# Graph attention over 64 graphs: a new order on four engines and in the DMA queue

## The reference, cut to what matters

```
h = relu(layernorm(x))                                   # x: 64 x 128 x 384
q, k, v = h @ Wq + bq, h @ Wk + bk, h @ Wv + bv          # 12 heads of 32
scores = q @ k.T / sqrt(32) + beta * adj                 # adj: 64 x 128 x 128, shared by the heads
scores = where(adj > 0, scores, -9e15)
out = x + softmax(scores) @ v
```

## Time and profile before

| | |
|---|---|
| median of 3 runs | 549.69 us (548.75 to 551.79) |
| the profiled execution's own time | 552.24 us |
| its span, first to last instruction | 550.4 us |
| granted clock of TensorE, mean | 0.991 of full speed |
| busy: PE, DVE, ACT, POOL | 504.8, 469.1, 443.3, 127.4 us |
| moved by DMA | 106.19 MB, mean 193 GB/s |

### The profile page before, as it was taken

How to read it: one execution, slowest core, us unless ns; L and a number is a source line. 1 busy time by engine, 2 the same in 40 slices (tenths; PEclk the granted TensorE clock), 3 DMA queues, 4 the chain that set the end, 5 groups by cost and what they waited for, 6 DMA issues and landing times.

```text
span 550.4 us, 17259 instructions
## 1 busy us (share of the span) xinstructions
PE 504.8 (92%) x5142; PEld 417.6 (76%) x5142; DVE 469.1 (85%) x2323; ACT 443.3 (81%) x1816; POOL 127.4 (23%) x204
## 2 busy tenths in 40 slices
PE   8998897887999989899998989989898999999986
PEld 7776776765887878688787878868786887888774
DVE  5687697967899899889989989889997998887796
ACT  3567687786697969879796997879798797989885
POOL 5411021212122222212222222222222221111131
PEclk9999999999899999989999999999999999999999
DMA  8424465656577667767766775776667566644311
GB/s 256 155 88 153 132 222 164 214 194 210 168 231 232 222 214 231 231 184 231 233 221 219 239 226 174 234 234 221 219 230 233 172 197 213 193 154 149 107 59 58
DMA packets 111959, 106.19 MB, mean 193 GB/s; under 512 B 12448, under 2 KB 97312, under 8 KB 111904
## 3 DMA queue, kind: packets, MB, share of 16 engines
q1 hardware_dynamic: 111904, 105.56, 59.6%
HBM read 55.84 MB, written 49.68 MB: 192 GB/s over the span
## 4 chain that ended last, share of the span: by engine, by line
SPq 30%; DMA 27%; PE 18%; DVE 8%; issue 7%; ACT 1%; DVEq 0%
DMA out_rows<-out_blocks 14%; SPq L425 12%; DMA probs_rows<-probs_blocks 10%; SPq L454 7%; PE G_ps L906 7%; SPq L401 6%; PE S_ps L975 4%; SPq L416 3%; DMA probs_moved<-probs_rows 3%; PE S_ps L927 2%; DVE probs L737 2%; PE PT_ps L959 2%; PE PT_ps L943 2%; SPq L393 1%; ACT probs L538 1%
## 5 line engine op out<-in xcount | busy, mean ns | idle before, releaser
L538 ACT ACTIVATE probs<-probs,negmax 128x128 f32<-128x128 f32 x532 | 206.1, 397 | 0.0
L737 DVE CUSTOM_DVE_ANT_0 probs<-S_ps,bias 128x128 f32<-128x128 f32 x768 | 166.1, 285 | 17.7 <-PE S_ps L927 17.4
L553 ACT ACTIVATE probs_blocks<-probs,negmax 128x128 f32<-128x128 f32 x236 | 92.0, 392 | 77.2 <-DVE negmax L737 67.1
L509 POOL TENSOR_TENSOR w_raw<-w_raw,x_ring 128x384 f32<-128x384 f32 x63 | 64.0, 1017 | 312.7 <-DVE w_raw L757 312.7
L906 PE MATMUL G_ps<-h_hi,w_hi 128*128 128x512 f32 x288 | 119.6, 415 | 0.0
L906 PE MATMUL G_ps<-h_hi,w_lo 128*128 128x512 f32 x288 | 118.6, 412 | 0.0
L906 PE MATMUL G_ps<-h_lo,w_hi 128*128 128x512 f32 x288 | 117.2, 407 | 0.0
L538 ACT ACTIVATION_READ_ACCUMULATOR probs<-probs,negmax 128x1 f32 x532 | 104.9, 197 | 0.0
L927 PEld LDWEIGHTS S_ps<-qk 32*128 32x128 f32 x1536 | 50.9, 189 | 38.0 <-issue 36.6
L927 PE MATMUL S_ps<-qk 32*128 32x128 f32 x1536 | 63.7, 294 | 15.7 <-DVE h_lo L676 10.4
L943 PE MATMUL PT_ps<-probsT,v 128*32 128x128 f32 x1512 | 54.7, 277 | 20.2 <-DVE probsT L778 13.9
(11 more groups left out here) (60 smaller groups left out, 725.6 us busy)
## 6 DMA issues: line engine op xcount, KB each, us to landing
probs_rows<-probs_blocks SPq DMA_DIRECT2D x59, 256.0 KB, 3.1
probs_moved<-probs_rows SPq DMA_DIRECT2D x236, 64.0 KB, 2.0
out_dram<-w_raw SPq DMA_DIRECT2D x63, 192.0 KB, 2.9
x_ring<-in_x_dram SPq DMA_DIRECT2D x61, 192.0 KB, 2.8
out_rows<-out_blocks SPq DMA_DIRECT2D x29, 384.0 KB, 3.3
w_raw<-out_rows SPq DMA_DIRECT2D x116, 96.0 KB, 2.2
xhat_rows<-xhat_blocks SPq DMA_DIRECT2D x26, 384.0 KB, 2.5
xhat_moved<-xhat_rows SPq DMA_DIRECT2D x104, 96.0 KB, 2.7
```

The source lines that it names most:

```text
L509: nc.gpsimd.tensor_tensor(y[:, place, :], y[:, place, :], x_ring[:, bass.ds(at, D)], ALU.add).then_inc(y_ready, 1)
L538: last = nc.scalar.activation(p, p, ACT.Exp, bias=negmax[:, e, j * KC + m:j * KC + m + 1], scale=TURN, accum_out=rowsum[:, e, m * HC + j:m ...
L553: last = nc.scalar.activation(blocks[:, j, :, :], probs[:, a, j, 0, :].rearrange("p (c e) -> p c e", c=HC), ACT.Exp, bias=negmax[:, a, j * ...
L737: last = nc.vector.tensor_tensor_reduce(probs[:, a, j, m, :], S_ps[:, j, m * N:(m + 1) * N], bias[(z.par + 1) % 2][:, z.s, :], 1.0, LARGES ...
```

## The change

It does these things:

- SP: the four reads of `out_rows` move from the end of an odd slot to the next even slot, behind the four reads of `probs_rows`. The four reads of xhat blocks are split, two in each slot (`READS`). One x load moves from s = 2 to s = 1. The write of xhat rows stands behind the reads of xhat blocks.
- PE: the scores come first in every slot, then the first projection stretch, then the product with v (before: product with v directly behind the scores, and ahead of them where s = 0). In a group's last slot (`closing`) the second stretch comes ahead of the values, too.
- DVE: it stores no unit. `add_bv` moves to behind the mask terms, in the closing slot to behind `h_lo`; the quotient and the transpose of probs' blocks are last in the slot; the mask comes ahead of `store_outT` in every slot.
- ScalarE: it stores the sixth unit as well (`STORE_Q`), and `high_part` comes directly behind the exponentials of probs_blocks.

```diff
@@ -41,3 +41,5 @@
-LOADS = [[0], [1], [2, 3], []]
+LOADS = [[0], [1, 2], [3], []]
+READS = [[0, 1], [2, 3], [0, 1], [2, 3]]
 QK_UNITS = 6
@@ -48,8 +50,7 @@
-STORE_1 = [[], [1], [], [4]]
-STORE_2 = [[0], [], [3], []]
 STORE_0 = [[], [], [2], []]
-STORE_V = [[], [], [], [5]]
+STORE_1 = [[], [1], [], [4]]
+STORE_Q = [[], [], [], [5]]
+STORE_2 = [[0], [], [3], []]
@@ -176,4 +177,3 @@
         qk_in_psum = sem("qk_in_psum")
-        qk_stored_act, qk_stored_dve = sem("qk_stored_act"), sem("qk_stored_dve")
+        qk_stored = sem("qk_stored")
         mask_ready, bias_ready = sem("mask_ready"), sem("bias_ready")
@@ -230,2 +230,5 @@
                 first_f = n == NG and s == 0
+                self.pairs_before = 4 * (n - 1) + s - 2 > 0
+                self.first_f = first_f
                 self.moved = [2] * (not self.F and 4 * (n - 1) + s - 4 >= 0) + [2, 1] * first_f
@@ -235,3 +238,4 @@
-                self.scores_first = self.A and self.P and s > 0
+                self.closing = self.P and s == GROUP - 1
                 self.par = off % 2
...
@@ -394,6 +390,6 @@
-            def read_blocks(pair):
+            def read_blocks(pair, columns):
                 at = pair * HC * RUN
-                for c in range(HC):
+                for c in columns:
                     came = xhat_rows[pair, :, c * RUN:(c + 1) * RUN].rearrange("(r p) n -> p r n", r=HC)
@@ -425,13 +421,21 @@
                         sp.dma_start(goes, came).then_inc(probs_blocks_moved[(z.s - 1) % 2], 16)
+                if z.W and z.s % 2 == 0 and z.pairs_before or z.first_f:
+                    sp.wait_ge(out_rows_written, 16 * z.pairs_written())
+                    for b in range(HC):
+                        came = out_rows[z.s // 2, :, b * SIX:(b + 1) * SIX].rearrange("(j p) n -> p j n", j=HC)
+                        goes = out_moved[b * HD:(b + 1) * HD, z.s // 2, :].rearrange("p (j n) -> p j n", j=HC)
+                        sp.dma_start(goes, came).then_inc(out_blocks_moved[z.s // 2], 16)
                 load_ahead(z)
-                if not (z.static and not 1 <= z.groups(0) <= NG - 3):
-                    if z.s % 2 == 1:
-                        sp.wait_ge(xhat_ready, order(z.count(2)) + 1)
-                        write_rows(z.s // 2)
-                    if z.s == 2:
-                        sp.wait_ge(rows_written[0], 16 * z.groups(0))
-                        read_blocks(0)
+                xhat_here = not (z.static and not 1 <= z.groups(0) <= NG - 3)
+                if xhat_here and z.s == 2:
+                    sp.wait_ge(rows_written[0], 16 * z.groups(0))
+                if xhat_here and z.s >= 2:
+                    read_blocks(0, READS[z.s])
                 if z.M and z.s == 0:
                     sp.wait_ge(rows_written[1], 16 * z.groups(-1))
-                    read_blocks(1)
+                if z.M and z.s < 2:
+                    read_blocks(1, READS[z.s])
+                if xhat_here and z.s % 2 == 1:
+                    sp.wait_ge(xhat_ready, order(z.count(2)) + 1)
+                    write_rows(z.s // 2)
                 if z.W and z.s % 2 == 1:
@@ -448,8 +452,2 @@
                     sp.dma_start(out[bass.ds(z.o - d, 1), :, :].rearrange("b t d -> t (b d)"), y[:, place, :]).then_inc(out_written[place], 16)
-                if z.W and z.s % 2 == 1:
-                    sp.wait_ge(out_rows_written, 16 * (z.pairs_written() + 1))
-                    for b in range(HC):
-                        came = out_rows[1 - z.s // 2, :, b * SIX:(b + 1) * SIX].rearrange("(j p) n -> p j n", j=HC)
-                        goes = out_moved[b * HD:(b + 1) * HD, 1 - z.s // 2, :].rearrange("p (j n) -> p j n", j=HC)
-                        sp.dma_start(goes, came).then_inc(out_blocks_moved[1 - z.s // 2], 16)
                 if z.L:
@@ -567,9 +565,8 @@
                     act.wait_ge(scores_in_psum, z.count(-1) - z.s)
-                stored = qk_stored_dve if u == QK_UNITS - 1 else qk_stored_act
                 if u < KC:
                     nc.scalar.activation(qk[z.par][:, u, :], G_ps[:, u % 2, :], ACT.Identity, bias=bq_scaled[:, u:u + 1],
-                                         scale=TURN * SCALE).then_inc(stored, 1)
+                                         scale=TURN * SCALE).then_inc(qk_stored, 1)
                 else:
                     nc.scalar.activation(qk[z.par][:, u, :], G_ps[:, u % 2, :], ACT.Identity,
-                                         bias=bk_col[:, u - KC:u - KC + 1]).then_inc(stored, 1)
+                                         bias=bk_col[:, u - KC:u - KC + 1]).then_inc(qk_stored, 1)
@@ -611,2 +608,7 @@
                     exponentials_ahead(z)
+                if z.M:
+                    high_part(z)
+                if z.P:
+                    for u in STORE_Q[z.s]:
+                        store_qk(z, u)
                 if z.E and not z.F:
@@ -617,6 +619,4 @@
                     store_probsT(z, 2)
-                if z.M:
-                    high_part(z)
                 if z.P:
-                    for u in STORE_2[z.s] + STORE_V[z.s] * (z.static and z.groups(0) == 0):
+                    for u in STORE_2[z.s]:
                         store_qk(z, u)
...
@@ -813,7 +799,5 @@
                     return
-                if z.F and z.A:
-                    mask(z)
                 if z.O and not z.F:
                     reciprocals(z)
-                if z.scores_first:
+                if z.A:
                     mask(z)
@@ -821,4 +805,2 @@
                     store_outT(z)
-                if z.A and not z.F and not z.scores_first:
-                    mask(z)
                 if z.M:
@@ -829,8 +811,7 @@
                     reciprocals(z)
-                for d in z.moved:
-                    quotient(z, d)
-                if z.A:
+                if z.F:
+                    for d in z.moved:
+                        quotient(z, d)
+                if z.F and z.A:
                     add_bv(z)
-                if z.R:
-                    transpose_probs(z)
                 if z.F and z.A:
@@ -861,2 +842,4 @@
                         mask_terms(z)
+                        if z.A and not z.closing:
+                            add_bv(z)
                     statistics(q, s)
@@ -872,5 +857,9 @@
                     normalise(z, q)
-                if z.P and not first:
-                    for u in STORE_V[z.s]:
-                        store_qk(z, u)
+                if z.A and z.closing:
+                    add_bv(z)
+                if not z.F:
+                    for d in z.moved:
+                        quotient(z, d)
+                if z.R:
+                    transpose_probs(z)
                 if first and z.s == GROUP - 1:
@@ -899,7 +888,4 @@
-                    if u == 1:
-                        if started(z.stored_dve()):
-                            pe.wait_ge(qk_stored_dve, z.stored_dve())
-                    elif started(z.stored_act(u - 2)):
-                        pe.wait_ge(qk_stored_act, z.stored_act(u - 2))
+                    if started(z.units(u - 1)):
+                        pe.wait_ge(qk_stored, z.units(u - 1))
                 for n in range(first, last):
@@ -918,3 +904,3 @@
                 if z.s == 0:
-                    pe.wait_ge(qk_stored_act, z.stored_act(-2))
+                    pe.wait_ge(qk_stored, z.units(0))
                 ts = slice(z.s * N, (z.s + 1) * N)
@@ -922,4 +908,2 @@
                 for m in range(KC):
-                    if z.s == 0 and m == KC - 1:
-                        pe.wait_ge(qk_stored_dve, z.stored_dve())
                     for j in range(HC):
@@ -1027,7 +1011,3 @@
                         warm(WARM[GROUP])
-                if z.A and z.scores_first:
-                    scores(z)
-                if z.O:
-                    probs_times_v(z)
-                if z.A and not z.scores_first:
+                if z.A:
                     scores(z)
@@ -1036,2 +1016,7 @@
                         project(z, *part)
+                if z.O:
+                    probs_times_v(z)
+                if z.closing:
+                    for part in STRETCH_2[z.s]:
+                        project(z, *part)
                 if z.A:
@@ -1044,3 +1029,3 @@
                     transpose_probs(z, 2)
-                if z.P:
+                if z.P and not z.closing:
                     for part in STRETCH_2[z.s]:
```

More of the change, by code:

```diff
@@ L47 @@
 STRETCH_2 = [[(0, 7, 9), (1, 0, 4)], [(2, 2, 9)], [(3, 7, 9), (4, 0, 5)], [(5, 3, 9)]]
+STORE_0 = [[], [], [2], []]
 STORE_1 = [[], [1], [], [4]]
+STORE_Q = [[], [], [], [5]]
 STORE_2 = [[0], [], [3], []]
-STORE_0 = [[], [], [2], []]
-STORE_V = [[], [], [], [5]]
 WARM = [8, 2, 2, 3, 7]
@@ L694, in mask_bias @@
                                                in1=mask_term[:, :], op0=ALU.mult, op1=ALU.add).then_inc(bias_ready, 1)
-            def store_qk(z, u):
-                dve.wait_ge(qk_in_psum, z.units(u + 1))
-                if started(z.count(-1) - z.s):
```

(9 more changed lines are left out.)

4 lines of the change are left out of this document (removed).

## The result

The changed kernel takes 582.01 us (median of 4 runs, 579.9 to 584.59) against 549.22 us for the kernel before on the same chip: a ratio of 1.0596, 95% interval 1.0531 to 1.0662. It is slower, as forecast, but by 5.96% and not by 2.2%, and outside the range (546 to 572).

The account below looks back on a forecast made before the run. SP's closed queue loop was taken as the bound. Issue and landings gave 32.53 us against 31.62, with an edge 1.0 more a group; 11 groups plus 1.0 made plus 12 on 549.69, so 561.6 us, range 546 to 572.

Parts of the forecast that it names:

- SP's closed loop sets the period: SP's queue: probs_rows write, landing, reads and other issue form one loop, 31.62 us a group, however early PE or DVE are.
- Issue, 20.15 us a group: SP's queue: the issue parts of four slots after the change, 5.58, 5.52, 5.37 and 3.68 us, together 20.15.
- The moved reads lose their cover, 0.7 us an odd slot: Out reads on SP: some 0.7 us of their issue lay inside the probs_rows wait; moved, 1.87 us is paid openly.
- The landing shortens by about 0.45 to 3.45.: The probs_rows write in s=1: its landing, 3.9 us before, was to shorten by about 0.45 to 3.45 us.
- Base: The starting period of SP's loop, 31.62 us, summed from one middle group of the earlier trace.
- Ramp and tail: 0: Start and end of the kernel: no cost, with ends of both signs under 1 us.
- group 14 plus 1.0: Group 14, without xhat writes: PE's loop decides there and adds 1.0 us.
- The other edits: 0: Reordering on PE, DVE and ScalarE: slack outside SP's loop, worth 0 while that loop is the longer one.
- The output store is covered: Even slots: store issued by 7.8 us, probs_rows lands at 8.16; covered by 0.4 us, so priced 0.
- the faster one: Odd landings fall to 2.6 us, SP needs 30.8 a group, 0.8 less; 542 us in all, chance 0.13.
- that of no change: Odd landings of 3.0 us give 31.6 a group, as now; about 551 us, chance 0.13.
- The third rival: Output store loses its 0.4 us cover; each even slot 0.5 us longer, another 1.0 a group, 573 us, chance 0.14.

Follow-up runs that it names:

- e3: The changed kernel with its one x load moved back from s=1 to s=2; 582.74 us, ratio 1.057 to the kernel before.
- e5: The changed kernel with the x load back in s=2 and the xhat reads whole in the even slots; 574.41 us, ratio 1.041 to the kernel before.
- e8: The kernel before with x and adj loads and xhat reads moved behind the write of probs_rows, issued while it lands; 534.02 us, ratio 0.969.
- e1: The changed kernel with SP's program of before, the other engines as changed; 558.55 us, ratio 1.016 to the kernel before.
- e6: The changed kernel with the out reads, in even slots, ahead of the wait for probs_rows and its four reads; 563.75 us, ratio 1.022 to the kernel before.
- e2: The kernel before with SP's loads, reads and slot as changed, the other engines as before; 590.87 us, ratio 1.074.
- e12: The changed kernel with probs_rows written ahead of the two 384 KB writes in odd slots; 556.28 us, ratio 1.010 to the kernel before.
- e11: The changed kernel with the last pair's out reads back ahead of the last output store of the ring part; 581.0 us, a single run.
- e7: The changed kernel with SP's program of before and DVE's quotient back in the middle of its slot; 553.14 us, ratio 1.006 to the kernel before.

## Why the prediction was wrong, by its steps

- **SP's closed loop sets the period.** Right. Before, after, and in e3 to e5, the time from a write of probs_rows to its reads is the landing to within 0.06 us in the slots where nothing else is waited for; taking issue out of the loop made the kernel 17 us faster (e8), and SP's old program with the changed engines brought 24 of the 33 us back (e1).
- **Issue, 20.15 us a group.** Right: 20.19.
- **The moved reads lose their cover, 0.7 us an odd slot.** Right: 1.25 us a group and 18 us in all, by e6.
- **"The landing shortens by about 0.45 to 3.45."** This step failed. It lengthened by 0.8, to 4.70. It was worked out so: 384 KB more ahead of the write would take 1.05 us, SP's longer issue would give the engines 1.49 us more to work them off, so the write would find less in front of it. It did not. From its issue to its landing in s=1 the engines moved 1.45 MB, against 1.46 before, so the longer issue had bought nothing; and they moved it at 309 GB/s and not at 373, since they were partly idle at both ends, above all in the last 0.9 us. A full queue's rate was priced for a stretch that was not full. Its bound was wrong with it: I had taken the 3.9 us of before as the upper end, though the queue had got 384 KB more ahead of the write. The missed 1.25 us in each of 8 groups are 10 us, of the 15.4 by which the forecast was short in the profiled executions (20 by the medians). e2 shows the late landing with the changed queue alone, e5 and e12 show that what stands ahead of the write matters; why the last engines finish so late is open.
- **Base.** The one group in the earlier trace rows takes 31.62 us; the mean of eight is 32.11. The forecast used a difference, so this alone cost nothing.
- **"Ramp and tail: 0", group 14 plus 1.0.** Wrong: 2.1 us before group 1, 5.0 in groups 13 and 14, 4.0 at the end; against that, groups 1 to 4 took 0.3 more and not 3. I had seen that the last pair's reads come later and priced it under 1; it is 3.4 (e11), as the store ahead of it waits for the quotient. Of the 5.0 in groups 13 and 14, e6 gives 3.2 back. The ramp's 2 us come mostly with the engines' order (e1 and e7 reach group 1 at 33.9 and 33.6 us, e2 at 32.4).
- **The other edits: 0.** Wrong in both directions: minus 7 to 9 us with the changed queue, plus 8 with the old one, plus 9.5 with a short one. Calling it slack that "moves no L425" missed that the moved quotient takes DVE's wait off its other work, and that SP does wait for DVE and ScalarE where that work is late (13.4 and 3.9 us in e2).
- **The output store is covered.** Right for the changed kernel in most slots (wait s=3 0.3 us over the landing), thin as I had it: with the shorter landing of e12 it was the longest wait of the queue.

The rivals: the faster one (which the passage on lighter load calls the second) and that of no change are out; the landing in s=1 went away from 2.6 and that in s=3 stayed (3.38 and 3.39 us). The third rival's sign was nearer, but its mechanism is hardly there: in the even slots SP's wait is the landing to within 0.02 us, and the store adds 0.3 in s=3.

## What to carry to other kernels

Where one queue waits for a landing in each round, add up the round: issue, landing, issue. What is issued between a write and the wait for it was free here, and what is issued behind the wait was paid, as long as nothing else held the queue; moving four reads from the one to the other cost 18 us, and moving loads the other way saved 17, less than the issue that was moved, since other waits came up. A removed wait is no gain if the next wait of the same queue was running under it. And a landing that is not in the trace in its new neighbourhood has no upper bound in the old one: if more is queued ahead of it, let the range go beyond the longest seen. When you compare two rates of a queue, put both windows where it is full, and look at its ends apart.

## What had not been expected of the hardware

- A write of 256 KB landed 2.0 us after its issue where the loads stood behind it (e8, s=0), 2.6 to 2.9 on average in the even slots of the kernels before and after, 3.4 behind two writes of 384 KB, and 4.2 to 5.6 where adj, two x loads and two sets of small reads were queued as well.
- With 256 KB behind two writes of 384 KB, the middle of the stretch from issue to landing ran at 398 GB/s in one order of DMAs and at 380 in the other. What differed most was its end: in the last 0.9 us the DMA engines were busy to a share of 0.83 before and of 0.40 after.
- The first wide matmul behind a run of small tiles takes about 0.11 us longer than the next one (0.50 and 0.39 behind the scores, 0.45 and 0.34 behind the product with v), and the change the other way costs 0.09 more (0.32 and 0.23 start to start).
